# State sums by fp32 transposes in PSUM, gating after the turn, and contiguous gate/up tiles in a four-stage layer kernel

## What is computed

```
x = x + attention_mix(layernorm(x), ctx)          # softmax(QK^T) of ctx, applied to x
x = x + moe(layernorm(x))                         # 16 experts, top 2, F = 192: down(silu(g) * u)
x = x + selective_scan(ctx, z = layernorm(x))     # below
x = x + two_experts(layernorm(x))                 # 2 of 8 experts chosen over all tokens, 2048 wide

# selective_scan, per channel d (512) and state n (16), over time l (512):
state = state * exp(dt * A[d, n]) + dt * u * B[n, l]
y     = sum over n of state * C[n, l]
y     = (y + D[d] * u) * silu(z)
```

## Time and profile before

| | |
|---|---|
| median of 3 executions | 1737.92 us (1737.42 to 1743.07) |
| the profiled execution's own time | 1745.28 us |
| its span in the trace | 1743.2 us |
| PE busy | 85% of the span |
| DVE / ACT / POOL busy | 57% / 37% / 44% |
| mean granted PE clock | 0.907 of full speed |
| mixture stage, three passes | about 417 to 868 us |
| combine stage | 868 to about 1003 us |
| last experts' products | about 1010 us to the end |
| DMA | 191.10 MB, 112236 packets, of which 62600 under 2 KB |

### The profile page before, as it was taken

How to read it: one execution, slowest core, us unless ns; L and a number is a source line. 1 busy time by engine, 2 the same in 40 slices (tenths; PEclk the granted TensorE clock), 3 DMA queues, 4 the chain that set the end, 5 groups by cost and what they waited for, 6 DMA issues and landing times.

```text
span 1743.2 us, 18297 instructions
## 1 busy us (share of the span) xinstructions
PE 1485.5 (85%) x5472; PEld 1001.5 (57%) x5472; DVE 989.8 (57%) x1258; ACT 647.2 (37%) x1191; POOL 772.6 (44%) x567
## 2 busy tenths in 40 slices
PE   6988862667998899799915569999999999999998
PEld 3444432323454455445404558787878787878786
DVE  2767768899787689678768521424242424142422
ACT  4445531334454345344402223333333333333332
POOL 0000004476566467467266134444454445444443
PEclk9899875789999899899955579999999999999999
DMA  3220225026768867876464292001000100010000
GB/s 96 99 98 25 73 91 199 28 72 206 230 208 255 267 205 220 263 250 207 134 205 165 112 352 94 13 0 61 0 12 0 60 0 12 0 40 8 0 0 24
DMA packets 112236, 191.10 MB, mean 110 GB/s; under 512 B 10600, under 2 KB 62600, under 8 KB 110656
## 3 DMA queue, kind: packets, MB, share of 16 engines
q1 hardware_dynamic: 98880, 157.03, 26.8%
q0 software_dynamic: 6400, 20.98, 3.9%
q10 hardware_dynamic: 6912, 12.59, 2.4%
HBM read 152.55 MB, written 38.01 MB: 109 GB/s over the span
## 4 chain that ended last, share of the span: by engine, by line
PE 69%; DVE 11%; DMA 6%; issue 6%; POOL 4%; ACT 2%; SPq 2%; ACTq 0%; POOLq 0%; DVEq 0%
PE decay L1629 20%; PE bank L1618 19%; PE bank L1485 7%; PE bank L1505 6%; DMA WGU<-in_L_ffn_up_w 5%; DVE decay L1158 4%; PE bank L1523 3%; PE bank L1427 2%; PE decay L1383 2%; POOL Y L714 1%; PE bank L1390 1%; DVE XH L1024 1%; POOL ZT L723 1%; PE bank L1498 1%; PE bank L1447 1%
## 5 line engine op out<-in xcount | busy, mean ns | idle before, releaser
L1340 DVE CAST HFH<-HF 128x512 fp32r<-128x512 f32 x128 | 58.9, 460 | 497.7 <-ACT HF L955 497.7
L674 POOL TENSOR_TENSOR S<-DTU,Bb 128x1024 f32<-128x1024 f32 x128 | 298.9, 2356 | 69.0 <-PE bank L1485 61.2
L764 POOL TENSOR_TENSOR W2L<-W2R,W2H 128x512 fp32r<-128x512 f32 x128 | 172.2, 1346 | 349.1 <-ACT W2H L950 349.1
L1158 DVE TENSOR_TENSOR_SCAN decay<-decay,S 128x1024 f32<-128x1024 f32 x128 | 293.0, 2289 | 2.3 <-ACT decay L841 2.3
L1485 PE MATMUL bank<-S,ident 128*128 128x512 f32 x512 | 248.5, 615 | 37.0 <-DVE DTU L1174 23.6
L1618 PE MATMUL bank<-XSH,W1H 128*128 128x512 f32 x512 | 203.1, 397 | 4.2 <-POOL W1L L760 4.2
L1629 PE MATMUL decay<-W2H,HFH 128*128 128x512 f32 x512 | 200.4, 391 | 5.3 <-DVE HFL L1342 5.3
L1618 PE MATMUL bank<-XSH,W1L 128*128 128x512 f32 x512 | 203.2, 397 | 0.0
L1618 PE MATMUL bank<-XSL,W1H 128*128 128x512 f32 x512 | 202.6, 396 | 0.0
L1629 PE MATMUL decay<-W2L,HFH 128*128 128x512 f32 x512 | 199.9, 390 | 0.0
L1629 PE MATMUL decay<-W2H,HFL 128*128 128x512 f32 x512 | 199.7, 390 | 0.0
(11 more groups left out here) (204 smaller groups left out, 1974.6 us busy)
## 6 DMA issues: line engine op xcount, KB each, us to landing
WGU<-in_L_ffn_gate_w SPq DMA_DIRECT2D x48, 384.0 KB
WGU<-in_L_ffn_up_w SPq DMA_DIRECT2D x48, 384.0 KB
WD<-in_L_ffn_down_w SPq DMA_DIRECT2D x48, 384.0 KB, 3.3
Bb<-bc_rows SPq DMA_DIRECT2D x32, 512.0 KB, 7.1
Cb<-bc_rows SPq DMA_DIRECT2D x32, 512.0 KB, 8.8
expert_rows<-YT ACTq DMA_DIRECT2D x48, 256.0 KB
W1R<-in_L_ffn_w SPq DMA_DIRECT2D x8, 1024.0 KB, 14.1
W2R<-in_L_ffn_w SPq DMA_DIRECT2D x8, 1024.0 KB, 14.1
```

The source lines that it names most:

```text
L674: pool.tensor_tensor(S[j][:], DTU[:, ds(b, 1), c, :].to_broadcast([P, PAIR, L]), Bb[j][:], ALU.mult).then_inc(dbu_ready, 1)
L764: pool.tensor_tensor(W2L[f % 2][:], W2R[:, ds(e, 1), f, :].rearrange("p e d -> p (e d)"), W2H[f % 2][:].bitcast(F32), ALU.subtract).then_i ...
L1158: dve.tensor_tensor_scan(flat, flat, S[j][:].rearrange("p i l -> p (i l)"), 0.0, ALU.mult, ALU.add).then_inc(scan_done, 1)
```

## The change

Four things are changed.

- **State sums.** S is now the stationary operand and the identity the moving one, in transpose mode: eight transposes of 128 x 128 per unit (2 states x 4 token tiles) that accumulate in YS. A chunk's y then stands in YS turned: tokens on partitions, and for each token tile 128 channels side by side.
- **Skip term.** ACT scales u by D in place (scale_u), and after a chunk's last unit PE adds it to YS by four more transposes; a semaphore us_ready says that it is scaled. take_y is now a plain copy of YS to DTU on ACT. load_u stands in step 2 instead of step 3, behind a wait for the last sum of the sequence before.
- **Gating.** PE turns silu(z) itself (turn_gated waits for zt_ready). DVE multiplies the turned tile in PSUM by the turned y from DTU into X3 and adds the residual in a second operation. POOL's product is gone (rstd_of_z).
- **Weight tiles.** WGU is [P, 2, K, F]: each load writes one run of K * F = 768 words per partition, and the up product reads its two halves from two places.

```diff
-        WGU = [sb(f, f"WGU{i}", [P, K, 2, F]) for i in range(2)]
+        WGU = [sb(f, f"WGU{i}", [P, 2, K, F]) for i in range(2)]
@@ SP, load_expert and mixture_steps
-                sp.dma_start(w[:, :, 0, :], gate_w[ds(e, 1)].rearrange("e (p k) f -> (e p) k f", p=P)).then_inc(gu_loaded[n % 2], DMA)
-                sp.dma_start(w[:, :, 1, :], up_w[ds(e, 1)].rearrange("e (p k) f -> (e p) k f", p=P)).then_inc(gu_loaded[n % 2], DMA)
+                sp.dma_start(w[:, 0], gate_w[ds(e, 1)].rearrange("e (p k) f -> (e p) k f", p=P)).then_inc(gu_loaded[n % 2], DMA)
+                sp.dma_start(w[:, 1], up_w[ds(e, 1)].rearrange("e (p k) f -> (e p) k f", p=P)).then_inc(gu_loaded[n % 2], DMA)
...
-                    if n == 3:
-                        sp.wait_ge(y_ready, b * DC)
+                    if n == 2:
+                        sp.wait_ge(s_summed, b * UB)
                         load_u(b)
@@ POOL, combine stage
-            def rstd_and_gate(b):
+            def rstd_of_z(b):
                 pool.wait_ge(var2_ready, b + 1)
                 pool.tensor_tensor(rstd[:], vare[:], minus_half[:], ALU.pow).then_inc(rstd2_ready, 1)
-                for c in range(DC):
-                    wait_apart(pool, zt_ready, b * DC + (c + 1))
-                    pool.tensor_tensor(ZT[:, c, :], ZT[:, c, :], DTU[:, ds(b, 1), c, :].rearrange("p b l -> p (b l)"),
-                                       ALU.mult).then_inc(gate_ready, 1)
@@ ACT
+            def scale_u(b, c):
+                if c == 0:
+                    act.wait_ge(ul_loaded, b * DMA + DMA)
+                act.activation(U[:, c, :], U[:, c, :], ACT.Copy, scale=skip[:, c:c + 1]).then_inc(us_ready, 1)
+            def take_y(b, c):
+                wait_apart(act, s_summed, b * UB + (c + 1) * NP)
+                act.copy(DTU[:, ds(b, 1), c, :].rearrange("p b l -> p (b l)"), YS[:]).then_inc(y_ready, 1)
...
                     decay(b, 2 * n + 1)
                     copy_ht(j0, n)
+                    if n == 1:
+                        take_y(b - 1, DC - 1)
+                    elif n % (NP // 2) == 1:
+                        take_y(b, n // (NP // 2) - 1)
+                    if 3 <= n < 3 + DC:
+                        scale_u(b, n - 3)
@@ DVE: take_y and its calls are gone; combine
-                    dve.tensor_tensor(X3[:, t, :], PS[t][:], X2[:, t, :], ALU.add).then_inc(x3_ready, 1)
+                    dve.tensor_tensor(X3[:, t, :].rearrange("p (c d) -> p c d", c=DC),
+                                      PS[t][:].rearrange("p (c d) -> p c d", c=DC),
+                                      DTU[:, ds(b, 1), :, t * P:(t + 1) * P].rearrange("p b c d -> p (b c) d"),
+                                      ALU.mult).then_inc(gated, 1)
+                for t in range(T):
+                    dve.wait_ge(gated, b * T + (t + 1))
+                    dve.tensor_tensor(X3[:, t, :], X3[:, t, :], X2[:, t, :], ALU.add).then_inc(x3_ready, 1)
@@ PE, add_states
-                    ins = pe.matmul(YS[:], ident[:], S[j][:, i, :], start=(j + i == 0),
-                                    stop=(j == NP - 1 and i == PAIR - 1))
+                    for t in range(T):
+                        ins = pe.matmul(YS[:, t * P:(t + 1) * P], S[j][:, i, t * P:(t + 1) * P], ident[:],
+                                        start=(j + i + t == 0), stop=False, is_transpose=True, skip_group_check=True)
+                if j == NP - 1:
+                    pe.wait_ge(us_ready, b * DC + c + 1)
+                    for t in range(T):
+                        ins = pe.matmul(YS[:, t * P:(t + 1) * P], U[:, c, t * P:(t + 1) * P], ident[:],
+                                        start=False, stop=True, is_transpose=True, skip_group_check=True)
```

More of the change, by code:

```diff
@@ L332, in build_program @@
         s_summed = sem("s_summed")
+        us_ready = sem("us_ready")
         y_ready = sem("y_ready")
@@ L361, in build_program @@
         zt_ready = sem("zt_ready")
-        gate_ready = sem("gate_ready")
+        gated = sem("gated")
         gt_ready = sem("gt_ready")
@@ L733, in combine_pool @@
                 if ahead > 0:
-                    rstd_and_gate(b + 1)
+                    rstd_of_z(b + 1)
                 if ahead > 1:
@@ L744, in _ @@
             gather_y(1, 0, Y1, 3)
-            rstd_and_gate(0)
+            rstd_of_z(0)
             pool.wait_ge(x2_ready, T)
@@ L872, in _ @@
                 decay(0, u)
+                if u % NP == NP // 2:
+                    scale_u(0, u // NP)
+                if u % NP == 3 and u > NP:
+                    take_y(0, u // NP - 1)
             act.wait_ge(slots_ready, 1)
@@ L905, in _ @@
             mixture_steps(B - 1, True)
+            take_y(B - 1, DC - 1)
             def silu_z(b):
@@ L1167, in read_out @@
                 dve.tensor_tensor(S[j][:], DA[j % 2][:], Cb[j][:], ALU.mult).then_inc(hc_ready, 1)
[L1169 to L1175, removed]
             def gate_h(j0, n):
@@ L1190, in _ @@
                 scan(0, u)
-                if u % NP == 2 and u > NP:
-                    take_y(0, u // NP - 1)
                 read_out(0, u)
@@ L1202, in mixture_steps @@
                     scan(b, 2 * n)
-                    if n == 1:
-                        take_y(b - 1, DC - 1)
-                    elif n % (NP // 2) == 1:
-                        take_y(b, n // (NP // 2) - 1)
                     read_out(b, 2 * n)
@@ L1223, in _ @@
             mixture_steps(B - 1, True)
-            take_y(B - 1, DC - 1)
             def statistics(src, norm, ready):
@@ L1504, in up @@
                 for k in range(K):
-                    ins = pe.matmul(UP[:, 0:2 * F], XGT[n % 2][:, k, :],
-                                    WGU[n % 2][:, k].rearrange("p g f -> p (g f)"), start=(k == 0), stop=(k == K - 1))
+                    ins = pe.matmul(UP[:, 0:2 * F].rearrange("p (g f) -> p g f", g=2), XGT[n % 2][:, k, :],
+                                    WGU[n % 2][:, :, k, :], start=(k == 0), stop=(k == K - 1))
                 ins.then_inc(up_ready, 1)
@@ L1567, in turn_gated @@
                 for c in range(DC):
-                    pe.wait_ge(gate_ready, b * DC + (c + 1))
+                    pe.wait_ge(zt_ready, b * DC + (c + 1))
                     for t in range(T):
```

## The result

The changed kernel takes **1681.26 us** (median of 4 executions, 1678.71 to 1687.49) against 1737.70 for the kernel before in the same session: ratio 0.9638, 95% interval 0.9599 to 0.9676. It is faster by 56 us; the forecast was 1666 us, in a range of 1648 to 1696. The profiled execution has a span of 1680.6 us (before 1743.2), 62.6 us less.

What follows compares the result with a forecast made beforehand. PE was taken as the bound of the 8.43 us regular step, DVE next. Terms 27.5 + 25 + 6 + 13 = 71.5 us off 1745.3 gave 1673.8, hence a median of 1666 us, range 1648 to 1696.

Steps and rivals of the forecast that it cites:

- State sums, 27.5 us: Regular steps: transposes replace two products per sum, saving 1.10 us a step over 25 steps, 27.5 us.
- DVE is late next: Regular steps: with PE shortened to 6.87 or 7.34 us, DVE's 7.33 us sets the step.
- Weight tiles, 2.4 us per tile: Gate/up weight loads: 3072-byte rows instead of 768 take 2.1 us of all DMA engines per tile, not 4.5.
- Rival C: Weight loads: packets no cheaper, or the queue sets the landing; a border saves 5 us, the start 3; 1684 us; chance 0.13.
- Borders, 25 us: Eight steps around each border between passes: shorter steps 8 x 1.10 plus 3.7 us, 12.5 us each, 25 for two.
- Rival B: Borders between passes: waits for weights nearly vanish and the clock stays up, 11 us less per border, 1645 us; chance 0.13.
- The first pass's first steps, 6 us: First four steps of the first pass: counted as half a border, 6 us saved.
- Skip term, take_y, prologue, 0: ACT's scale and copy per chunk stay covered, and prologue gains and half-clock losses cancel: together zero.
- Gating, 13 us: Combine stage: POOL loses 16 x 1.478 us, DVE gets 10.9 us of products; net 14.7 us, taken as 13.
- The median: Whole kernel: profiled execution was 7.4 us above the median 1737.9, so 1673.8 us became a forecast median of 1666.
- Rival E: Every step: PE's clock falls because transposes count as idleness; step 9.2 us, kernel slower at 1759 us; chance 0.05.
- Rival D: State sums: transposes take 0.2 us each, PE's step 8.2 us, kernel 1710 us; chance 0.05.

Runs made afterwards that it cites:

- the version with U spread out: Changed kernel with gate/up weights issued ahead of the down weights and U's load moved out of the border into steps 5 and 9: 1652.23 us, 0.9460 of the kernel before.
- the control: The changed kernel unaltered, measured again in five more rounds beside the kernel before: ratio 0.9634 (0.9593 to 0.9675).

## Why the prediction was right, and where it was wrong

**State sums, 27.5 us: right in mechanism, undersized.** The transposes were taken at 0.94 us and took 0.87; "DVE is late next" at 7.33 us was 7.31, gapless, and a copy put back on DVE lengthened its step to 7.76. The term measured 35.3. It counted 25 steps where 27 were regular (2.2 us), and it took 7.33 for every step. After a border PE is behind DVE and catches up at its own pace: products 22 to 25 follow at 6.85 to 6.88 us, so the 27 steps average 7.16. That is 4.6 us. (Where PE never waited for weights, as in the version with U spread out, there was nothing to catch up, and the steps took 7.31.) The last us is the step from product 4 to 14, which was 8.53 on average before, not 8.43.

**Weight tiles, 2.4 us per tile: the step that failed.** I drew a line through two 1 us windows, 414 GB/s with 4096-byte rows and 185 with 768-byte rows, and read the second as the price of small packets. The second was misread: of the 83 packets in 568 to 569 us only 43 are under 2 KB, the other 40 are larger rows, so 70 ns a row was no row's time. A longer stretch gives 50.5 us of engine time per MB for both tiles, and the same kernel with either tile differs by 2% and 3.8% in engine time, where the forecast had more than twice as much per byte. Rival C had this mechanism at 1684 us, and the measured 1681 is nearest to it, with borders at 5 us each against the measured 2.1 and 4.9 (7.6 and 6.7 in the control); the reason I gave against C, that the order shows one run of 768 words, says nothing on cost. The tiles did help, by 8 us in the kernel before, and the earlier end of the issue is the likely way; in the changed kernel it shows in the regular steps, with their 6 us of lead, in the kernel before in the first steps and borders (6.7 us, one execution each).

**Borders, 25 us: wrong by 18, in the control's execution by 11.** The four waits were forecast at 0.8, 6.8, 0.4 and 0, and U's at 1.2; they came at 6.31, 9.25, 4.34 and 0, and U's at 1.42. I had the term that works against the gain, "PE wants back" the 1.10 us a step, but took it once per wait, beside a full 8 x 1.10 us of gain from shorter steps. Of these 17.6 us and the 7.4 for cheaper packets the two borders kept 7.1 (14.3 in the control): what the steps lost came back as waits for weights. I had seen the 2 MB in front of the longest wait without adding up the border, 23 MB at a share of 0.85. Bytes were not all of it: the same bytes went through in 70 us once the weights were issued ahead, and with U moved out as well a border is 66 to 67 us at a share of 1.01. So the step that failed here is the 8 x 1.10: in a border the pace was set by when the weights were asked for and what stood in front of them, not by PE's step. How the two share the time isn't parted by any run. Rival B, that the waits vanish, is refuted by the same rows. The first pass's first steps, 6 us, are the same kind of stretch and gave 0.2. U's load cost 1.42 us at this border, but 0.19 at the other and 2.93 in the control, so that the 1.2 I had put is near one of the three only.

**Skip term, take_y, prologue, 0: right.** ACT's operations stayed hidden; product 0 starts 0.6 us later and runs at half clock (5.10 us where it took 2.85), as the prediction said.

**Gating, 13 us: right in mechanism, undersized.** Waits 11.8 (13.0 measured), normalisations 10.8 (12.4), the end 3 (2.9), DVE's new products 10.9 (9.9). The end came at another place than forecast. Before, DVE's last product follows its normalisations without a gap (976.50), so POOL was hidden there; but PE's last turns waited for POOL (to 975.79) and pushed PE's products for the routing back, so that PE took up the last normalised tile 3.56 us after DVE began it (986.86 - 983.30), and 0.61 us after in the changed kernel. Not seen: add_first beside POOL, 2.6 us. The sum of 14.7 was then cut to 13 for no row's sake; 20.4 came. Two terms that I priced apart hang together: moving the gating took away the waits and brought the time back as slower add_first and late turned tiles; taking the work off POOL did pay.

**The median.** The terms missed by 9 us (71.5 forecast, 62.6 measured on the spans). The other 6 come from taking 7.4 us off for the distance between the profiled execution and the median: the profiled execution after is only 1.5 us above its own.

**Rival E**, the clock falling in each step, is refuted: PEclk 1.00 in 750 to 800 us, with 16 to 20 transposes of S and U in every step, and 2.2 to 2.7 us at a time with nothing but transposes on PE. The Trainium skill, TensorE: Matmul & The Clock Gate, Part 4 (PE-mode transpose), says that full clock does not engage for transpose mode; in this row it holds through them. That transposes alone also raise it rests on the one place of the earlier trace rows. Rival D (0.2 us each) is refuted by 0.109; plain products, at 0.224, would have been it.

## What to carry to other kernels

Before a step is made shorter, add up the bytes that each stretch moves and read its DMA share. Here, in borders with a share of 0.85 and waits for weights, much of what the steps lost came back as longer waits (the two borders kept 7 us in one execution and 14 in the other, where shorter steps alone should have brought 17.6), and the gain was to be had from the order in which the queue asks. A load stands in the queue behind every wait ahead of it; split a group of loads whose buffers come free at different times. And an operation on POOL can cost DVE its full duration where both work in SBUF, so its price is not read from its own engine.

## What was not expected

- POOL's tensor products and DVE's add_first exclude each other: 7.75 us together, where add_first alone takes 2.74 and POOL's products 4.93, and one DVE operation of 0.75 us stood for 5.75. In the mixture stage POOL's products for S run beside DVE's scans in every step, and the scans keep their 2.29 us; a scan has one of its operands in PSUM, add_first both in SBUF. Whether that is the reason was not tested.
- An fp32 transpose of 128 x 128 that accumulates in PSUM takes 0.109 us at full clock, one record each; the same product without the mode takes 0.224 us and two records.
- Loads with 768-byte and 3072-byte rows cost the engines nearly the same (50.5 us per MB in two regular stretches, 2% and 3.8% more for the small rows over two pairs of whole runs), but issuing the pair takes 1.32 us against 0.82.
- The order of SP's queue alone was worth 21 us with every byte still moved, and with U moved 30 us: 1652.23 us.
